# A graph network on one core: two small loads change their places in SP's order

## The chip, the cores and the metric

The kernel runs on 1 core of one Trainium2 chip. The metric is device time in microseconds of one execution, median of several; less is better.

## The reference

Two graph layers over 6250 nodes with 128 features and 106,250 edges (sorted by destination, both directions of 50,000 random pairs, and a loop at each node):

```python
h = max(layernorm(x), 0)
msg = edge_weight * (h @ W_i [dst] + h @ W_j [src] + edge_attr @ W_e)
x = x + segment_sum(msg, dst) + h @ W_self
h = max(layernorm(x), 0)
for W_l, b, W_r in two layers:          # relu between them, log_softmax behind the second
    mean = segment_sum(h[src], dst) / max(count(dst), 1)
    h = mean @ W_l.T + b + h @ W_r.T
out = x + h
```

## The kernel before

Nodes are laid out in 49 blocks of 128 (BLOCKS), worked on in 7 steps of 7 blocks (STEPS, UNROLL), a step in a part of 4 and one of 3 blocks.

The edge phase runs over 64 chunks of 1664 edges. GpSimd gathers source rows, VectorE builds one-hot matrices, TensorE sums them by destination (L1030). On the way TensorE also counts, for every group of destinations, how often each source occurs (L1039); ScalarE copies the counts and SP stores them in DRAM (`counts`, L502). The degree and the sum of edge weights of every node go to `node_rows` (L490). For each block the product h @ W_i (the "own" rows) is stored in `own_rows` (L494).

Then comes the passage in which this case's change lies. A node's own row has to be multiplied by its sum of edge weights. SP loads the sums as 49 rows of 128 values (L512) into `node_weight_rows`, TensorE transposes them (L1127), ScalarE copies them to `node_weight` (L865). SP loads the own rows back in two parts, of 2 and of 5 steps (`OWN_PARTS`, L517; 7168 and 17,920 B in each of 128 partitions), and GpSimd multiplies them block by block (L684, 49 instructions). For each step VectorE adds the own rows (L1537) and TensorE's mix (L931, added by L1542) to x and works out the layer norm (L1231, L1234); ScalarE normalizes (L720) and makes the high halves in f16 (L727), VectorE the low halves (L1522); TensorE turns the rows (L920). On TensorE L1127 stands ahead of all mixes. On VectorE this is `first_rows`; behind it stand the maximum and the reciprocal of the degrees (L1620, L1622, semaphore `inv_made`). SP stores the reciprocals in `inv_row` (L535), waits for the store and loads them back broadcast to 128 partitions (L527, `load_inverse`).

The two passes of the second layer (PASSES 1 and 2) don't gather. Each multiplies the node features by the stored counts in 18 "supers" of 98 matmuls (L1120, `sum_super`): super k needs 4287.5 KB of counts in `ring[k % 2]` (L523, `load_counts`), and behind it VectorE scales the sums by `inv_deg[k % 2]` (L1582, `keep_sums`). `ring[0]` and `deg_lines` lie where the gathered rows were; `ring[1]` and both `inv_deg` lie over the accumulators that the mixes read, so they wait for the last mix (`mixed[0]` at 49). For k from 2 on, SP issues the counts when super k - 2 has ended and the inverse when VectorE has read it. Behind super 0 of pass 1 TensorE turns the last two steps (L1135), VectorE copies them (L1349), and super 1 waits for these copies and for its counts.

SP issues every load and store of this passage in program order, each behind its waits.

Of the kernel before, what the change touches and what calls it, by code (L numbers as in the profile page):

```python
# [5 lines left out]
P = 128  # L6
NODES, EDGES, FEATS = 6250, 106250, 128
BLOCKS = -(-NODES // P)
USED = BLOCKS * P
TILES = 13  # L10
CHUNK = P * TILES
CHUNKS = -(-EDGES // CHUNK)
# [101 lines left out]
def gnn_program(nc, x, src, src_batches, dst, dst_lines, prev_lines, src_lines, factor_lines, edges, weights, biases, out):  # L114
# [12 lines left out]
    def scratch(name, shape, dt=f32):  # L127
        return nc.dram_tensor(name, shape, dt, kind="Internal").ap()
# [5 lines left out]
    node_rows = scratch("node_rows", (2, COUNTED * NCHUNK))  # L134
# [8 lines left out]
    with ctx:  # L143
# [6 lines left out]
        def sem(name):  # L150
            return ctx.enter_context(nc.semaphore(name))
# [29 lines left out]
        def carve(home, taken, width, dt=f32, partitions=P):  # L181

            taken[0] += width
            assert taken[0] <= home.shape[1]
            part = home[0:partitions, taken[0] - width:taken[0]]
            return part if dt is f32 else part.bitcast(dt)
# [41 lines left out]
        in_h, in_N = [0], [0]  # L228
# [7 lines left out]
        w_half = carve(accN, in_N, P // 2, f16)  # L236
        own_h = [carve(accN, in_N, FEATS) for _ in range(2)]
        own_hT = carve(accN, in_N, P)
        assert in_N[0] <= USED
        node_weight_rows = accN[0:BLOCKS, USED:USED + P]  # L240
        def ghot(k):
            at = k * GW
# [89 lines left out]
        weight_in, weight_turned, weight_kept = sem("weight_in"), sem("weight_turned"), sem("weight_kept")  # L332
# [28 lines left out]
        node_out = [sem(f"node_out{b}") for b in range(2)]  # L361
# [14 lines left out]
        mixed = [sem(f"mixed{p}") for p in range(3)]  # L376
# [42 lines left out]
        def _(sp):  # L419
# [52 lines left out]
            for i, c in enumerate(ORDER):  # L472
                b = i % 2
# [13 lines left out]
                if c < COUNTED:  # L487
# [4 lines left out]
                    t = i - OWN_MADE  # L492
# [14 lines left out]
            fast = sp.value_load(fast_row[0:1, 0:1], min_val=0, max_val=1)  # L507
            with sp.If(fast):

                for b in range(2):  # L510
                    sp.wait_ge(node_out[b], 16 * (CHUNKS // 2 - b))
                sp.dma_start(node_weight_rows, node_rows[0, 0:USED].rearrange("(t p) -> t p", p=P)).then_inc(weight_in, 16)  # L512
                sp.wait_ge(own_out, 16 * BLOCKS)
                sp.wait_ge(piece_done, DSUPERS * PIECES)
                for n, (lo, hi) in enumerate(OWN_PARTS):
                    columns = slice(lo * UNROLL * FEATS, hi * UNROLL * FEATS)
                    sp.dma_start(accN[:, columns], own_rows[:, columns]).then_inc(own_back[n], 16)  # L517

                for h in range(2):
                    sp.wait_ge(counts_out[h], 16 * COUNTED)  # L520
                sp.dma_start(deg_lines, node_rows[1, :].rearrange("(p n) -> p n", p=LINES)).then_inc(deg_in, 16)
                def load_counts(p, k):
                    sp.dma_start(ring[k % 2].rearrange("p (c n) -> p c n", c=SUPER),  # L523
                                 counts[k * SUPER:(k + 1) * SUPER, :, :].rearrange("c p n -> p c n")).then_inc(ring_in[p][k % 2], 16)

                def load_inverse(p, k):
                    sp.dma_start(inv_deg[k % 2], inv_row[k * SNODES:(k + 1) * SNODES].rearrange("(a n) -> a n", a=1)  # L527
                                 .to_broadcast([P, SNODES])).then_inc(inv_in[p][k % 2], 16)

                sp.wait_ge(added[0], ADDED)  # L530
                load_counts(1, 0)
                sp.wait_ge(mixed[0], BLOCKS)
                load_counts(1, 1)
                sp.wait_ge(inv_made, 2)
                sp.dma_start(inv_row.rearrange("(p n) -> p n", p=LINES), deg_lines).then_inc(inv_out, 16)  # L535
                sp.wait_ge(inv_out, 16)
                for p in PASSES:
                    if p == 1:
                        load_inverse(1, 0)
                        load_inverse(1, 1)  # L540
                    else:

                        sp.wait_ge(super_done[1], SUPERS - 1)
                        load_counts(2, 0)
                        sp.wait_ge(super_read[1], SUPERS + 1)
                        load_inverse(2, 0)
                        sp.wait_ge(super_done[1], SUPERS)
                        load_counts(2, 1)
                        sp.wait_ge(super_read[1], SUPERS + 2)
                        load_inverse(2, 1)  # L550
                    for k in range(2, SUPERS):

                        sp.wait_ge(super_done[p], k - 1)
                        load_counts(p, k)
                        sp.wait_ge(super_read[p], k + 1)
                        load_inverse(p, k)
# [659 lines left out]
        def _(dve):  # L1216
# [137 lines left out]
            def load_window(c):  # L1354
                _, (more, base) = nc.values_load_multi_w_load_instructions(
                    win_row[0:1, bass.ds(c, 1), :].rearrange("a c n -> a (c n)"), engines=[dve.engine], min_val=0, max_val=NODES - 1,
                    skip_runtime_bounds_check_because="both were clamped to these bounds when the row was written")
                dve.reg_mov(next_more, more)
                dve.reg_mov(next_base, base)
# [76 lines left out]
            def window_base(c):  # L1436
                _, (base,) = nc.values_load_multi_w_load_instructions(
                    win_row[0:1, c, 1:2], engines=[dve.engine], min_val=0, max_val=NODES - 1,
                    skip_runtime_bounds_check_because="it was clamped to these bounds when the row was written")
                return base  # L1440
# [342 lines left out]
```

## Time and profile before

| | us |
|---|---|
| median of 3 executions | 1657.07 |
| lowest, highest | 1655.46, 1662.93 |
| the profiled execution | 1655.46 |
| its span, first to last instruction | 1653.7 |
| TensorE (PE) busy | 1416.1 |
| VectorE (DVE) busy | 977.2 |
| GpSimd (POOL) busy | 727.3 |
| ScalarE (ACT) busy | 601.3 |

The profile shows one execution. Times in rows are microseconds from the span's start unless marked ns. PE is TensorE, PEld its weight loads, DVE VectorE, ACT ScalarE, POOL GpSimd; SPq is the queue from which SP issues transfers. L12 is line 12 of the kernel.

### The profile page before, as it was taken

The page shows a single profiled execution, that of the slowest core. Times are in us where ns is not written, and L with a number is a line of the kernel's source. Part 1 is how long each engine was busy: PE and PEld are TensorE (multiplying, and loading weights), DVE is VectorE, ACT ScalarE, POOL GpSimd, SP SyncE. Part 2 cuts the span into 40 slices and gives each one's busy share as a digit, 9 for nine tenths or more (in the row PEclk, how much of TensorE's full clock was granted, in tenths as well). Part 3 has the DMA queues.
Part 4 walks back from the last instruction along what each step waited for, and adds up shares of the span by engine and source line. Part 5 has one row for each costly group of instructions (what it writes and reads, how often), then busy time and mean ns, then how long its engine had stood idle before and what let it go on. Part 6 is the DMA issues. An engine that isn't in the chain of part 4 may idle for free.

```text
span 1653.7 us, 25952 instructions
## 1 busy us (share of the span) xinstructions
PE 1416.1 (86%) x8448; PEld 1011.7 (61%) x8449; DVE 977.2 (59%) x4423; ACT 601.3 (36%) x1479; POOL 727.3 (44%) x783
## 2 busy tenths in 40 slices
PE   2587787888887988979899777899999979999997
PEld 0365666666665766657566556566666656666664
DVE  7798988898897987979799566300101130010204
ACT  5356556655646465554544234300000010020203
POOL 8777755665767766677677768000000000000000
PEclk9688988999998999989899899999999989999999
DMA  8467767988998888888799864586767647777773
GB/s 268 145 221 270 256 241 252 328 283 268 303 312 281 286 300 265 289 295 290 260 319 322 253 214 189 227 309 263 301 262 301 262 186 289 271 309 269 304 275 137
DMA packets 178853, 441.26 MB, mean 267 GB/s; under 512 B 24619, under 2 KB 104924, under 8 KB 175388
## 3 DMA queue, kind: packets, MB, share of 16 engines
q1 hardware_dynamic: 155996, 391.75, 65.5%
q0 software_dynamic: 22432, 46.97, 10.4%
q8 instruction: 70, 1.15, 0.3%
q10 hardware_dynamic: 288, 0.85, 0.1%
q14 instruction: 67, 0.55, 0.1%
HBM read 318.94 MB, written 120.55 MB: 266 GB/s over the span
## 4 chain that ended last, share of the span: by engine, by line
PE 60%; POOL 10%; DVE 9%; DMA 8%; ACT 7%; issue 4%; SPq 1%; DVEq 0%; POOLq 0%; ACTq 0%
PE psAE L1120 32%; PE psAE L1030 13%; POOL home L630 8%; DMA home<-h_table 6%; PE psAE L1062 4%; ACT home L789 3%; PE psW L931 3%; DVE home L1420 3%; DVE home L1424 2%; PE psW L1049 2%; PE psW L1039 2%; DVE home L1478 2%; ACT home L821 1%; DMA counts<-home 1%; PE psNS L1039 1%
## 5 line engine op out<-in xcount | busy, mean ns | idle before, releaser
L630 POOL DMA_INDIRECT home<-h_table,src_i x676 | 654.6, 968 | 289.4 <-issue 199.0
L1120 PE MATMUL psAE<-home 128*128 128x350 f16 x3528 | 538.1, 313 | 5.7 <-DVE home L1522 3.7
L1120 PEld LDWEIGHTS psAE<-home 128*128 128x128 f16 x3528 | 337.8, 96 | 200.9 <-issue 3.7
L1030 PE MATMUL psAE<-home 128*128 128x256 f32 x1352 | 331.4, 405 | 45.9 <-DMA home<-h_table,src_i 24.7
L1030 PEld LDWEIGHTS psAE<-home 128*128 128x128 f32 x1352 | 274.1, 205 | 102.8 <-issue 55.9
L1478 DVE TENSOR_SCALAR home<-iota_h,dst_rel,home 128x128 f32<-128x128 f16 x832 | 221.4, 361 | 30.4 <-PE psAE L1030 27.9
L789 ACT ACTIVATE home<-psW 128x490 f16<-128x490 f32 x418 | 211.5, 577 | 59.3 <-PE psW L1039 33.6
L1420 DVE TENSOR_SCALAR home<-iota_h,tile 128x245 f16<-128x245 f16 x1004 | 208.8, 298 | 30.1 <-PE psW L1049 16.5
L1424 DVE TENSOR_SCALAR home<-iota_h,tile 128x128 f16<-128x128 f16 x1004 | 178.3, 278 | 0.0
L1039 PE MATMUL psW<-home 128*128 128x245 f16 x836 | 126.9, 283 | 38.1 <-DVE home L1424 35.6
L1582 DVE SCALAR_TENSOR_TENSOR home<-psAE,home 128x350 f32<-128x350 f32 x18 | 9.4, 523 | 242.9 <-PE psAE L1120 238.1
L1582 DVE SCALAR_TENSOR_TENSOR home<-psAE,unscale,home 128x350 f32<-128x350 f32 x18 | 10.5, 581 | 238.4 <-PE psAE L1120 238.4
L1062 PE MATMUL psAE<-home 128*128 128x400 f32 x294 | 121.9, 561 | 26.0 <-DMA home<-h_table 25.8
L768 ACT ACTIVATE home<-psAE 128x256 f32<-128x256 f32 x52 | 20.0, 385 | 321.1 <-PE psAE L1030 321.1
L789 ACT ACTIVATE home<-psNS 128x490 f16<-128x490 f32 x212 | 110.4, 577 | 32.4 <-PE psNS L1039 22.5
L1039 PEld LDWEIGHTS psW<-home 128*128 128x128 f16 x836 | 80.1, 101 | 67.0 <-issue 26.7
L880 ACT ACTIVATE home<-home x14 | 8.0, 575 | 283.1 <-DVE home L1559 263.7
L1062 PEld LDWEIGHTS psAE<-home 128*128 128x128 f32 x294 | 59.4, 214 | 70.8 <-DMA home<-h_table 32.1
L1467 DVE TENSOR_SCALAR home<-iota_h,home 128x128 f16<-128x128 f16 x240 | 57.6, 327 | 54.7 <-PE psW L1049 43.8
L1039 PE MATMUL psNS<-home 128*128 128x245 f16 x424 | 68.0, 286 | 19.1 <-DVE home L1424 12.4
L821 ACT ACTIVATE home<-home 128x128 f16<-128x128 f16 x240 | 75.8, 393 | 0.0
L891 ACT ACTIVATE home<-home,shift (+1 forms) x49 | 18.9, 387 | 150.1 <-DVE shift L1589 150.1
(211 smaller groups left out, 1223.2 us busy)
## 6 DMA issues: line engine op xcount, KB each, us to landing
home<-counts SPq DMA_DIRECT2D x36, 4287.5 KB, 13.5
counts<-home SPq DMA_DIRECT2D x126, 612.5 KB
home<-edges SPq DMA_DIRECT2D x64, 845.0 KB
weighted<-home SPq DMA_DIRECT2D x24, 1225.0 KB
home<-weighted SPq DMA_DIRECT2D x36, 800.0 KB
home<-h_table,src_i POOLq DMA_INDIRECT x676
home<-h_table SPq DMA_DIRECT2D x36, 256.0 KB
home<-inv_row SPq DMA_DIRECT2D x36, 175.0 KB, 13.2
```

Source lines behind the costliest of these rows:

```text
L630: pool.indirect_dma_start(out=rows[to][:, j, :], out_offset=None, in_=from_table[:, :], in_offset=bass.IndirectOffsetOnAxis(ap=src_i[b][:, ...
L789: done = nc.scalar.activation(staged[h][:, :, at:at + 2 * GROUP], banks_of(i, "C", k)[u][:, 0:BCOLS].rearrange("p (d a) -> p a d", a=KEYS) ...
L821: done = nc.scalar.activation(whot_all[k % 2][:, j, 0, :], ghot(4 * k + j)[1], ACT.Copy, scale=w_parts[t][:, 0, at:at + 1])
L931: last = nc.tensor.matmul(bank[:, n * FEATS:(n + 1) * FEATS], frm[:, columns], w_sb[:, w, :], start=(k == 0), stop=(k == len(terms) - 1))
L1030: done = nc.tensor.matmul(psA[:, 0:2 * P].rearrange("p (n f) -> p n f", n=2), onehot[:, j, :], both_of(s, b, j), start=(j == 0), stop=(j = ...
L1039: done = nc.tensor.matmul(banks[j // 2][:, j % 2 * GCOLS:(j % 2 + 1) * GCOLS], residues, keys, start=True, stop=True)
L1062: done = nc.tensor.matmul(psE[:, 0:DNODES].rearrange("p (h d) -> p h d", h=2 * DSUPER), piece_h[b][:, a - n * PIECE, :], piece_w[b][:, :, ...
L1120: last = nc.tensor.matmul((psA, psE)[r][:, 0:SNODES].rearrange("p (c d) -> p c d", c=SUPER), halves[:, a, n, :], tiles[:, :, a, :], start= ...
L1420: nc.vector.tensor_scalar(ghot(k)[0], iota_h[:, 0:GCOLS], record_of(k, 0), None, ALU.is_equal)
L1424: last = nc.vector.tensor_scalar(ghot(k)[1], iota_h[:, 0:P], record_of(k, 2), None, ALU.is_equal)
L1467: last = nc.vector.tensor_scalar(whot_all[k % 2][:, j, 1, :], iota_h[:, 0:P], tile_of(t)[:, 2, at:at + 1], w_parts[t][:, 1, at:at + 1], AL ...
L1478: last = nc.vector.tensor_scalar(onehot[:, j, :], iota_h[:, 0:P], dst_rel[i % 2][:, j:j + 1], factor[i % 2][:, j:j + 1], ALU.is_equal, ALU ...
```

## The change

SP's order of issues in the passage changes in two places; no load, store, instruction or wait is added or dropped.

1. The load of the node weights, with its wait for the last stores of `node_rows`, moves from ahead of the two own-row loads to behind them.
2. For pass 1, the load of the counts of super 1, with its wait for the last mix, moves from ahead of the store of the inverse degrees to behind the first inverse load, so that the order is: inverse of super 0, counts of super 1, inverse of super 1.

An `assert` on the size of a region, which has no part in what runs, goes too.

```diff
@@ -236,7 +236,6 @@
-        assert in_N[0] <= USED
@@ -507,14 +506,14 @@
             with sp.If(fast):
 
-                for b in range(2):
-                    sp.wait_ge(node_out[b], 16 * (CHUNKS // 2 - b))
-                sp.dma_start(node_weight_rows, node_rows[0, 0:USED].rearrange("(t p) -> t p", p=P)).then_inc(weight_in, 16)
                 sp.wait_ge(own_out, 16 * BLOCKS)
                 sp.wait_ge(piece_done, DSUPERS * PIECES)
                 for n, (lo, hi) in enumerate(OWN_PARTS):
                     columns = slice(lo * UNROLL * FEATS, hi * UNROLL * FEATS)
                     sp.dma_start(accN[:, columns], own_rows[:, columns]).then_inc(own_back[n], 16)
+                for b in range(2):
+                    sp.wait_ge(node_out[b], 16 * (CHUNKS // 2 - b))
+                sp.dma_start(node_weight_rows, node_rows[0, 0:USED].rearrange("(t p) -> t p", p=P)).then_inc(weight_in, 16)
@@ -529,14 +528,14 @@
                 load_counts(1, 0)
-                sp.wait_ge(mixed[0], BLOCKS)
-                load_counts(1, 1)
                 sp.wait_ge(inv_made, 2)
                 sp.dma_start(inv_row.rearrange("(p n) -> p n", p=LINES), deg_lines).then_inc(inv_out, 16)
                 sp.wait_ge(inv_out, 16)
                 for p in PASSES:
                     if p == 1:
+                        sp.wait_ge(mixed[0], BLOCKS)
                         load_inverse(1, 0)
+                        load_counts(1, 1)
                         load_inverse(1, 1)
```

## Rows read from the trace of the kernel before

**Rows 1.** The page: span, and TensorE's busy time.

```profile
span 1653.7 us, 25952 instructions
PE 1416.1 (86%) x8448; PEld 1011.7 (61%) x8449; DVE 977.2 (59%) x4423; ACT 601.3 (36%) x1479; POOL 727.3 (44%) x783
```

**Rows 2.** Chain of waits, 985 to 1110 us: start, duration, what.

```profile
999.38 0.24 PE psAE L1127
...
999.96 8.76 POOL home L684 x14
1008.74 1.26 DVE x_sb L1537
...
1042.71 14.80 PE psAE L1120 x98
...
1060.46 0.56 DVE home L1349
1061.06 44.59 PE psAE L1120 x294
```

**Rows 3.** SP's issues, 984 to 1100 us: start, duration, line, transfer.

```profile
991.40 0.37 SPq L512 DMA_DIRECT2D home<-node_rows  x1
991.87 0.83 SPq L517 DMA_DIRECT2D home<-own_rows  x2
```

**Rows 4.** SP's issues, 1035 to 1060 us.

```profile
1039.91 0.38 SPq L523 DMA_DIRECT2D home<-counts  x1
1053.12 0.36 SPq L535 DMA_DIRECT2D inv_row<-home  x1
1054.60 0.83 SPq L527 DMA_DIRECT2D home<-inv_row  x2
1057.55 0.38 SPq L523 DMA_DIRECT2D home<-counts  x1
```

**Rows 5.** The two own-row loads (L517), from issue to landing.

```profile
DMA to landing us min/median/max: 5.9/8.4/10.9
```

**Rows 6.** All 36 counts loads (L523), from issue to landing.

```profile
DMA to landing us min/median/max: 13.0/13.5/15.0
```

**Rows 7.** Transfers issued from 1039 to 1042 us: KB, us to landing.

```profile
home<-counts SPq DMA_DIRECT2D x1, 4287.5 KB, 13.3
```

**Rows 8.** Transfers issued from 1054.5 to 1056 us.

```profile
home<-inv_row SPq DMA_DIRECT2D x2, 175.0 KB, 3.5
```

**Rows 9.** Transfers issued from 1058 to 1059 us.

```profile
home<-inv_row SPq DMA_DIRECT2D x1, 175.0 KB, 12.7
```

**Rows 10.** Packets by size, 992 to 993 us.

```profile
DMA packets 104, 0.22 MB, mean 216 GB/s; under 512 B 21, under 2 KB 66, under 8 KB 104
```

**Rows 11.** Packets by size, 993 to 996 us.

```profile
DMA packets 127, 0.88 MB, mean 292 GB/s; under 512 B 4, under 2 KB 8, under 8 KB 125
```

**Rows 12.** Packets by size, 1000 to 1001 us.

```profile
DMA packets 28, 0.50 MB, mean 502 GB/s; under 512 B 0, under 2 KB 0, under 8 KB 0
```

**Rows 13.** Packets by size, 1001 to 1002 us.

```profile
DMA packets 177, 0.24 MB, mean 237 GB/s; under 512 B 144, under 2 KB 144, under 8 KB 173
```

**Rows 14.** Windows between the passes: length, busy per engine, granted clock, DMA.

```profile
1344.00:1349.00 5.00, 0.94 (x4) 0.63 (x4) 2.20 (x7) 2.78 (x3) 0.00 (x0) 0.50 1.02 420
1349.00:1353.00 4.00, 4.00 (x17) 2.06 (x17) 4.00 (x5) 3.85 (x5) 0.00 (x0) 0.57 0.23 85
```

**Rows 15.** TensorE in order of time, 955 to 1045 us.

```profile
977.18 7.42 PE L1030 MATMUL psAE<-home 128*128 128x256 f32 x26 [4.91 <-DMA home<-h_table,src_i]
...
991.93 5.85 PE L1030 MATMUL psAE<-home 128*128 128x256 f32 x26 [3.13 <-DMA home<-h_table,src_i]
```

**Rows 16.** TensorE in order of time, 1040 to 1655 us.

```profile
1042.55 14.97 PE L1120 MATMUL psAE<-home 128*128 128x350 f16 x98
...
1059.11 0.98 PE L920 MATMUL psNS<-ident,home 128*128 128x128 f32 x7 [0.83 <-DVE home L1349]
...
1348.90 16.64 PE L1120 MATMUL psAE<-home 128*128 128x350 f16 x98 [3.69 <-DVE home L1522]
```

## Prediction

> **What bounds the kernel now.** I read the page first: TensorE is busy for 86% of a span of 1653.7 us [rows 1], so the question is where on TensorE's line the two edits fall. Both fall in the passage from the edge phase to the two passes over the stored counts, about 990 to 1076 us, and the chain of waits over that stretch says what releases what there [rows 2]. The transpose of the node weights on TensorE (L1127) runs at 999.38, GpSimd's multiplications of the own rows (L684) start at 999.96 and are the chain for 8.76 us (fourteen of them, the rows of the first two steps), VectorE takes over at 1008.74, and from there VectorE, ScalarE and TensorE hand each other seven steps until the first super starts at 1042.71. The second super starts at 1061.06, released by a copy on VectorE. After that TensorE runs supers of 14.8 us nearly back to back [rows 2, 16]. Whatever delays this passage is not won back later, because nothing behind it waits for anything but TensorE.
>
> Then the SP queue over the same stretch, since the edits only reorder SP's issues: node-weight load at 991.40, the two own-row loads from 991.87 [rows 3]; second counts load at 1039.91, the store of the inverse degrees at 1053.12, two inverse loads from 1054.60, third counts load at 1057.55 [rows 4]. Last, how long such loads take and in which order their packets run [rows 5 to 13].
>
> **Part 1: the node-weight load goes behind the own-row loads.** Nothing is added or removed; a load of 24.5 KB in 49 rows of 512 B is issued after 896 + 2240 KB instead of before them. All three conditions that SP waits for here are met before 991.4, so the waits themselves cost nothing in either order, and the own rows are issued 991.87 - 991.40 = 0.47 us earlier.
>
> What matters is when the small load lands. Packet sizes tell the order on the wire. From 992 to 993 there are 66 - 21 = 45 packets of 512 B to 2 KB, nearly all of the 49 rows of the node weights, while the own rows were already issued [rows 10]; from 993 to 996 nearly all packets are under 8 KB, the first own load with 7168 B a row [rows 11]; from 1000 to 1001 none is [rows 12], the second own load with 17,920 B a row; and the 200 B rows of the degree load, issued at 993.89, appear only from 1001 to 1002 [rows 13]. A small load waits for the large ones in front of it. The same is seen later: an inverse load lands 3.5 us after its issue on a free queue [rows 8] and 12.7 us behind a counts load [rows 9]. The own loads took 5.9 and 10.9 us [rows 5]; the second was issued at the end of a pair that took 0.83 us, about 992.3, and so landed at 1003.2. In the new order it lands some 0.5 us sooner, 1002.7, and the 49 rows, about a third of a microsecond of extra time, at about 1003.0. TensorE's L1127 then goes at about 1003.1 instead of 999.38: **3.7 us**. Queued behind it on TensorE is the whole first mix; behind it in data are ScalarE's copy, GpSimd's 49 multiplications and so VectorE. VectorE's second step is bound by GpSimd [rows 2], so nothing takes the delay up: the first super starts 3.7 us later. Bounds: nothing below 2.5 if the order on the wire holds (own packets end near 1001.0, less 0.5, plus 1 for the rows and 1 from last packet to landing), 4.5 above; 0 if it does not hold (a rival, below).
>
> The Trainium skill ("DMA: Bandwidth & Descriptors", "Why a DMA increments its semaphore by 16 and not by 1" and "Queues, rings and completion order") says that a load is spread over the largest number of engines up to 16 that divides its slowest dimension, which for 49 rows would be 7, and that completion isn't first in, first out per issuing engine. By that rule the small load could land ahead of the second own load, as soon as seven engines are through with their shares; an estimate by the page would be 1 us less than the 3.7. The trace agrees with ring order in [rows 10 to 13] and can't show which engines are used.
>
> **Part 2: the second counts load goes behind the inverse degrees.** Before, it is issued at 1039.91 and lands 13.3 us later [rows 4, 7], at 1053.2, 7.9 us ahead of its use at 1061.06. Afterwards SP first waits for VectorE's reciprocal, stores the row, waits for the store, issues one inverse load and only then the counts load, in the place that the second inverse load has now: the pair starts at 1054.60 and takes 0.83 us, so at about 1055.05. On a queue that is empty but for one inverse load it lands no sooner than 13.0, likely in 13.3 us [rows 6, 7]: 1055.05 + 13.3 = 1068.35. TensorE starts the second super 0.1 us later, at 1068.4 instead of 1061.06: **7.3 us**. Cover of 7.9 us is used up and 15.1 us of lateness is put in. All these times also carry part 1's 3.7 us, so the two add up.
>
> What is late next: the second inverse load, behind the counts load, is needed at the end of the second super, 15 us later, and lands at about 1069. The third counts load is issued at 1057.55 as now, runs behind the second for another 10.5 us or so and lands near 1080, before the second super can end at 1083. From there the queue is as before. VectorE's copies of the turned blocks and the first inverse load keep their times. The store L535 now finds a free queue, which it all but had. All of this costs nothing.
>
> **TensorE's clock.** TensorE ends the turns at 1060.1 [rows 16] and now idles 8.3 us. After the idle stretch between the passes the granted clock was 0.50 before and 0.57 for four microseconds after the restart, that is largely the 1.2 GHz level [rows 14], and that super took 16.64 us against 14.97 at full clock [rows 16]; after an idle of 4.9 us in the edge phase 26 matmuls took 7.42 against 5.85 us [rows 15]. So the second super loses **1.7 us** (bounds 0 and 1.7: nothing, if the clock holds). The idle of 4 to 5 us ahead of L1127 also may slow the first mixes; VectorE turns to the second mix only behind GpSimd's fourteen products, 1008.74 - 999.38 = 9.4 us after L1127, so I put it at 0, with 0.5 as the upper bound. The slow stretch at 1015 to 1021 may shift by as much either way.
>
> **Sum.** 3.7 + 7.3 + 1.7 = 12.7 us. The profiled execution took 1655.46 us (span 1653.7 and 1.8 around it) and is the lowest of three; its sum is 1668.2. Their median is 1657.07, 1.6 higher, which gives 1669.8. I forecast 1669.0.
>
> **Rivals.**
> - Both delays happen (the forecast): 0.80. With bounds: 2.5 + 7.0 + 0 = 9.5 to 4.5 + 7.5 + 2.2 = 14.2 us, that is 1665.0 on the profiled execution's scale to 1671.3 on the median's.
> - The node weights slip past the own rows and land before 999.38, by the rule cited or because the rows find a free engine. Then only 7.3 + 1.7 = 9.0 us remain, 7.3 without the clock's share: 1662.8 to 1666.1. For it speaks only that the small load is small; against it [rows 9, 10, 13]. 0.11.
> - The second and third counts loads share the engines instead of following each other. They are issued 2.5 us apart, so the second would land up to 8 us later: 20 us in all, 1676. [Rows 12, 13] show the loads one after the other, against it. 0.05.
> - The other side, faster: the counts load at 1039.91 runs through the first super; if it slows TensorE's and VectorE's accesses there, taking it away gives time back. The place is 1041 to 1053. The first super took 14.97 us with it, and its 98 matmuls run at 14.8 us in the chain [rows 2, 16], so they are not seen to be slowed. It decides only if it returns more than the 12.7 us lost out of a super of 15 us, and 8.3 more for faster by over 0.5%; if a super could run in no time at all, 12.7 - 14.8 would give 1655. 0.02.
> - The remaining 0.02 is for no effect: the counts load lands within 6.0 us of 1055.05, where the shortest of 36 took 13.0 [rows 6]; 1657.
>
> **How the numbers follow.** A measurement of this kernel tells about 0.5%, 8.3 us, from no change: 1665.4 is the border. The forecast case lies over it but for its lowest corner; the second straddles it, the third lies over it. Slower 0.80 x 0.98 + 0.11 x 0.5 + 0.05, about 0.89; within 0.5% 0.09; faster 0.02. The range takes in the second case's bottom and the forecast's top, and 2 or 3 us above for runs like the highest of the three: 1663 to 1674. Given the likeliest case alone I would say 1665 to 1672.
>
> **What the new profile would show.** Right: L1127 on TensorE near 1003, after an idle ended by a transfer; GpSimd's L684 starting 0.6 us later; first super about 3.7 us late; the second counts load issued near 1058.7 and landing after some 13.3 us; an idle of TensorE of about 8 us ended by a transfer from the counts, and a second super of 16.6 us; from the third super on everything late by the same 12.7 us. Wrong: L1127 at its old time (part 1's ring order), a landing of the counts load over 16 us (shared engines), or a second super of 15.0 us (clock).

## The result and the profile after

| | before | after |
|---|---|---|
| median of 6 executions, us | 1659.59 | 1673.70 |
| lowest, highest | 1655.17, 1665.42 | 1669.33, 1679.89 |
| the profiled execution, its span | 1655.46, 1653.7 | 1664.25, 1662.4 |

The ratio is 1.0081 with a 95% interval of 1.0053 to 1.0109: slower by 13.4 us (8.8 to 18.1). The kernel after is one line shorter, so its lines from 239 on carry smaller numbers, by 1 in most of what follows: L1126 is the old L1127, L1119 the old L1120.

The profiled execution of after is only 8.7 us longer than that of before. The reason lies ahead of the change: its edge phase ended 9.6 us sooner, the last turn of sums (old L1005, new L1004) being at 988.70 and not at 998.26. This end of the edge phase moves by some 20 us between executions of all the kernels below, so I count from there. Page of after:

```profile
span 1662.4 us, 25953 instructions
PE 1418.8 (85%) x8448; PEld 1013.4 (61%) x8449; DVE 979.4 (59%) x4423; ACT 600.4 (36%) x1479; POOL 727.2 (44%) x783
```

SP's issues of after, in order of time. They answer to [rows 3, 4]: own rows first, then the node weights; counts of super 1 only behind the store and the first inverse load.

```profile
985.21 0.85 SPq L513 DMA_DIRECT2D home<-own_rows  x2
986.15 0.36 SPq L516 DMA_DIRECT2D home<-node_rows  x1
...
1050.91 0.34 SPq L532 DMA_DIRECT2D inv_row<-home  x1
1052.37 0.36 SPq L526 DMA_DIRECT2D home<-inv_row  x1
1052.76 0.43 SPq L522 DMA_DIRECT2D home<-counts  x1
...
1057.19 0.38 SPq L522 DMA_DIRECT2D home<-counts  x1
```

TensorE of after, in order of time; in brackets the idle time before a row and what ended it.

```profile
988.70 0.44 PE L1004 MATMUL psAE<-ident,home 128*128 128x128 f32 x2 [0.47 <-ACT home L767]
996.32 0.34 PE L1126 MATMUL psAE<-ident,home 49*128 49x49 f32 x1 [7.18 <-DMA home<-node_rows]
...
1040.61 16.55 PE L1119 MATMUL psAE<-home 128*128 128x350 f16 x98
1057.00 0.93 PE L919 MATMUL psNS<-ident,home 128*128 128x128 f32 x7
1058.55 0.98 PE L919 MATMUL psNS<-ident,home 128*128 128x128 f32 x7 [0.62 <-DVE home L1348]
1068.19 42.09 PE L1119 MATMUL psAE<-home 128*128 128x350 f16 x268 [8.66 <-issue]
```

The same places in before:

```profile
998.26 0.44 PE L1005 MATMUL psAE<-ident,home 128*128 128x128 f32 x2 [0.47 <-ACT home L768]
999.38 0.23 PE L1127 MATMUL psAE<-ident,home 49*128 49x49 f32 x1 [0.68 <-issue]
...
1061.06 44.59 PE L1120 MATMUL psAE<-home 128*128 128x350 f16 x294 [0.96 <-DVE home L1349]
```

Both waits that were forecast are there. TensorE idles 7.18 us for the node weights (0.68 before, for nothing in particular), and 8.66 us ahead of super 1, where it idled 0.96. The second idle time is put down to "issue", but the transfers name it. Transfers issued from 1052.7 to 1053.1 us of after, with the time to landing:

```profile
home<-counts SPq DMA_DIRECT2D x1, 4287.5 KB, 15.3
```

1052.76 + 15.3 = 1068.06, and super 1 starts at 1068.19. The wire order of part 1 shows too. Packets of after from 994 to 995 us, then from 995 to 996:

```profile
DMA packets 28, 0.45 MB, mean 449 GB/s; under 512 B 1, under 2 KB 3, under 8 KB 3
```

```profile
DMA packets 251, 0.28 MB, mean 281 GB/s; under 512 B 162, under 2 KB 209, under 8 KB 249
```

Up to 995 it is the 17,920 B packets of the own rows; from 995 to 996 there are 209 - 162 = 47 packets of 512 B to 2 KB, the node weights, and L1126 follows at 996.32. Four windows of after: window, length, busy time of PE, PEld, DVE, ACT and POOL, then the granted clock (third number from the right), DMA share and GB/s:

```profile
1036.00:1040.00 4.00, 0.30 (x3) 0.28 (x3) 3.88 (x13) 3.96 (x9) 0.00 (x0) 1.00 0.01 2
1040.00:1044.00 4.00, 4.00 (x19) 2.31 (x18) 1.84 (x11) 3.31 (x9) 0.00 (x0) 0.57 0.00 0
1060.00:1068.10 8.10, 0.00 (x0) 0.00 (x0) 0.43 (x1) 0.00 (x0) 0.00 (x0) 0.56 0.99 404
1068.10:1072.00 3.90, 3.81 (x16) 2.10 (x17) 0.00 (x0) 0.00 (x0) 0.00 (x0) 0.60 1.02 419
```

Super 1 starts at a clock of 0.60, mostly the 1.2 GHz level. So does super 0 (0.57), which takes 16.55 us and not 14.97 as in [rows 16]. That of super 0 isn't the change's doing, as the experiments show: it is slow in most profiles of either order.

### The profile page after: what moved, and what is told of

The parts are those of the page before. It is cut to its first block and busy times, and to the rows that moved or that the text cites. A ratio compares the mean times of both kernels' runs of the same rounds, so it can differ in the third digit from the quotient of the medians.

```text
span 1662.4 us, 25953 instructions
## 1 busy us (share of the span) xinstructions
PE 1418.8 (85%) x8448; PEld 1013.4 (61%) x8449; DVE 979.4 (59%) x4423; ACT 600.4 (36%) x1479; POOL 727.2 (44%) x783
## 5 line engine op out<-in xcount | busy, mean ns | idle before, releaser
L1119 PE MATMUL psAE<-home 128*128 128x350 f16 x3528 | 541.3, 314 | 13.4 <-issue 8.7
L1119 PEld LDWEIGHTS psAE<-home 128*128 128x128 f16 x3528 | 339.1, 96 | 210.5 <-issue 12.6
L1029 PE MATMUL psAE<-home 128*128 128x256 f32 x1352 | 331.6, 406 | 44.1 <-DMA home<-h_table,src_i 20.1
L1477 DVE TENSOR_SCALAR home<-iota_h,dst_rel,home 128x128 f32<-128x128 f16 x832 | 222.6, 364 | 30.3 <-PE psAE L1029 27.8
L1419 DVE TENSOR_SCALAR home<-iota_h,tile 128x245 f16<-128x245 f16 x1004 | 208.9, 301 | 30.1 <-PE psW L1048 16.4
L1038 PE MATMUL psNS<-home 128*128 128x245 f16 x424 | 66.7, 282 | 21.5 <-DVE home L1423 18.5
L930 PE MATMUL psW<-w_sb,home 128*128 128x128 f32 x588 | 72.7, 284 | 0.8 <-DVE home L1581 0.8
## 6 DMA issues: line engine op xcount, KB each, us to landing
home<-counts SPq DMA_DIRECT2D x36, 4287.5 KB, 13.7
home<-inv_row SPq DMA_DIRECT2D x36, 175.0 KB, 13.5
```

What stands on the lines that cost most here:

```text
L930: last = nc.tensor.matmul(bank[:, n * FEATS:(n + 1) * FEATS], frm[:, columns], w_sb[:, w, :], start=(k == 0), stop=(k == len(terms) - 1))
L1029: done = nc.tensor.matmul(psA[:, 0:2 * P].rearrange("p (n f) -> p n f", n=2), onehot[:, j, :], both_of(s, b, j), start=(j == 0), stop=(j = ...
L1038: done = nc.tensor.matmul(banks[j // 2][:, j % 2 * GCOLS:(j % 2 + 1) * GCOLS], residues, keys, start=True, stop=True)
L1119: last = nc.tensor.matmul((psA, psE)[r][:, 0:SNODES].rearrange("p (c d) -> p c d", c=SUPER), halves[:, a, n, :], tiles[:, :, a, :], start= ...
L1419: nc.vector.tensor_scalar(ghot(k)[0], iota_h[:, 0:GCOLS], record_of(k, 0), None, ALU.is_equal)
L1477: last = nc.vector.tensor_scalar(onehot[:, j, :], iota_h[:, 0:P], dst_rel[i % 2][:, j:j + 1], factor[i % 2][:, j:j + 1], ALU.is_equal, ALU ...
```

## The experiments

Four stretches of the profiled executions tell more than the total. A is from the last turn of sums (L1005) to the node-weight transpose (L1127); B from there to super 0; C from the start of super 0 to the end of super 1 (SP issues a counts load at that moment); D is the rest. All in us, worked out as differences of starts.

| profiled execution | A | B | C | D | sum | ratio of times, 95% interval |
|---|---|---|---|---|---|---|
| before | 1.1 | 43.2 | 33.5 | 577.6 | 655.4 | |
| after | 7.6 | 44.3 | 44.0 | 577.8 | 673.7 | 1.0081 (1.0053 to 1.0109) |
| e1_weights_behind_own | 4.6 | 44.8 | 33.5 | 578.3 | 661.3 | 1.0043 (1.0021 to 1.0064) |
| e2_counts_behind_inverse | 1.2 | 44.1 | 44.3 | 577.8 | 667.4 | 1.0060 (1.0028 to 1.0092) |
| e3_weights_on_act_queue | 2.2 | 44.2 | 35.0 | 577.3 | 658.8 | 1.0035 (1.0015 to 1.0055) |
| e4_reciprocal_early | 1.1 | 44.0 | 34.6 | 578.6 | 658.4 | 1.0004 (0.9979 to 1.0028) |
| e5_idle_filled | 7.6 | 44.0 | 44.4 | 577.6 | 673.6 | 1.0081 (1.0052 to 1.0111) |
| e6_weights_between | 2.4 | 44.7 | 35.0 | 577.9 | 659.9 | 1.0005 (0.9981 to 1.0029) |
| e7_weights_behind_counts | 17.4 | 44.0 | 34.4 | 578.5 | 674.2 | 1.0070 (1.0046 to 1.0095) |
| e8_weights_act_queue_early | 2.1 | 44.8 | 35.0 | 577.6 | 659.4 | 1.0009 (0.9985 to 1.0033) |
| e9_idle_filled_36 | 8.0 | 44.3 | 43.2 | 578.3 | 673.8 | 1.0079 (1.0059 to 1.0098) |
| e10_first_step_on_vector | 1.2 | 41.4 | 33.5 | 578.4 | 654.5 | 0.9980 (0.9966 to 0.9995) |
| e11_reciprocal_early_and_vector | 1.1 | 40.1 | 34.5 | 578.7 | 654.4 | 0.9982 (0.9969 to 0.9995) |

All ratios are to before, run on the same chip. The chip of the last three runs took 2013.9 us for before (some 350 us more, all of it in the edge phase); only ratios and stretches are compared there.

**One edit at a time.** e1 has only the first edit, e2 only the second, as in the diff of the change.

> The first edit alone: the node-weight load behind the own-row loads, the counts of super 1 loaded early as before. Theory: transfers that SP issues run in order, so the 49 small rows wait for 3136 KB; TensorE idles ahead of L1127 until they land. L1127 runs 6 to 8 us after the last turn of sums (L1005) instead of 1.1 us; first super later by that and up to 1 us for the clock; super 1 starts 3.7 us behind the end of super 0 as before. Sum 4 to 8 us over before, ratio 1.002 to 1.005. Rival (the small load slips past): L1127 1.1 us behind L1005, ratio 1.000.

> The second edit alone: counts of super 1 behind the first inverse load, node weights in front as before. Theory: the load starts some 13 to 15 us later, its cover of 7.9 us is gone, TensorE idles about 8 us ahead of super 1, which then takes 16.4 us instead of 14.97 for the clock. L1127 1.1 us behind L1005. Sum 7.3 + 1.5 = 8.8 us over before, ratio 1.005. Rival (the second and third counts loads share the engines): landing over 16 us and ratio 1.01 or more. Rival (the load is covered anyway): 0.

TensorE of e1, in order of time:

```profile
997.57 0.44 PE L1005 MATMUL psAE<-ident,home 128*128 128x128 f32 x2 [0.48 <-ACT home L768]
1002.19 0.34 PE L1127 MATMUL psAE<-ident,home 49*128 49x49 f32 x1 [4.18 <-DMA home<-node_rows]
```

TensorE of e2:

```profile
1005.14 0.44 PE L1005 MATMUL psAE<-ident,home 128*128 128x128 f32 x2 [0.47 <-ACT home L768]
1006.29 0.23 PE L1127 MATMUL psAE<-ident,home 49*128 49x49 f32 x1 [0.70 <-issue]
...
1078.20 32.01 PE L1120 MATMUL psAE<-home 128*128 128x350 f16 x201 [8.45 <-issue]
```

Each edit brings its own wait and not the other's. By ratio e1 costs 7.2 us (3.5 to 10.7) and e2 10.0 us (4.7 to 15.3); together that is 17 against 13.4 measured for both, well within the intervals. In e1's profile L1127 comes 4.6 us behind L1005, 3.5 us more than in before, and not the 6 to 8 that I had read off after's profile.

**How far behind must the node weights be?** e6 puts their load between the two own loads, e7 behind the counts of super 0 too.

```diff
+# e6: inside the loop over OWN_PARTS, behind the own load of part 0
+if n == 0: wait node_out; sp.dma_start(node_weight_rows, ...)
...
 load_counts(1, 0)
+# e7: here instead
+wait node_out; sp.dma_start(node_weight_rows, ...)
```

> The node-weight load between the two own-row loads. Theory of order within the queue: it waits for 896 KB, not for 3136, and lands about 5 us sooner than behind both, near 6 us after its issue, which is at or before L1127's turn in executions where the last gather comes late. Cost against before 0 to 2 us, ratio 1.000 to 1.001; L1127 at most 2.5 us behind L1005. Rival (any place behind a large load costs the same, or none does): as the first edit alone, or as before.

> The node-weight load behind the counts load of super 0 as well. Theory of order within the queue: it waits for 4287.5 KB more and lands 14 to 16 us after the counts are issued, so L1127 stands 15 to 16 us behind L1005, and the time is 14 to 16 us over before, ratio 1.009. Rival (a small load slips past large ones): it lands 2 to 3 us after its issue, L1127 3 to 4 us behind L1005, ratio 1.001 to 1.002.

TensorE of e6 (lines up by one), then of e7:

```profile
1003.99 0.26 PE L1128 MATMUL psAE<-ident,home 49*128 49x49 f32 x1 [1.94 <-DMA home<-node_rows]
```

```profile
1018.51 0.34 PE L1127 MATMUL psAE<-ident,home 49*128 49x49 f32 x1 [16.91 <-DMA home<-node_rows]
```

SP's issues of e7:

```profile
1002.20 0.40 SPq L520 DMA_DIRECT2D home<-counts  x1
1002.69 1.49 SPq L531 DMA_DIRECT2D home<-node_rows  x1
```

24.5 KB issued at 1002.69 are used at 1018.51, 15.8 us later: the rival of a small load that slips past is dead within SP's queue. The load is used 6.0 us after its issue in e6 (issued at 998.00), 10.2 in after (986.15 to 996.32), 15.8 in e7, in step with the bytes ahead. The time of e7 is a miss in size: 11.7 us over before (7.7 to 15.8) where 14 to 16 were expected and stretch A shows 16.2, just outside the interval. The profiled execution doesn't explain it: the counts took 16.1 us to land there, and 14.3 (e3, e4) to 18.9 us (after) for the same load of super 0 in the other profiles, depending on how much of the own rows was still on the wire.

**Another queue.** In e3 and e8 ScalarE issues the load, in e3 behind its last copy of sums, in e8 ahead of it, once the last counts are stored:

```diff
+if i == CHUNKS - 1:  # e8, ahead of ScalarE's keep_sums; e3: at the head of ScalarE's last If(fast)
+    act.wait_ge(node_out[b], ...), act.wait_ge(counts_out[b], 16 * COUNTED)   # e3: node_out alone
+    act.dma_start(node_weight_rows, ...).then_inc(weight_in, 16)
```

> Own rows as in the first edit, but the node weights are loaded by ScalarE on its own queue behind its last copy of sums, a little before the last turn of sums. The own rows are then still on the wire. Theory of order within SP's queue: from another queue the load doesn't wait for them and lands 2 to 3 us after its issue, so L1127 stands 2 to 4 us behind L1005, and the time is 1 to 3 us over before, ratio 1.001. Rival (the 16 engines are full, whatever the queue): L1127 waits as in the first edit alone, 6 to 8 us, ratio 1.002 to 1.005.

> Own rows in SP's queue as in the first edit; the node weights are loaded by ScalarE on its own queue as soon as the last counts have been stored and ahead of its last copy of sums, about 2 us after SP has issued the own rows and while these are on the wire. Theory (the wait is for the same queue's order): the 512 B packets run among the own rows' packets, the load lands within 3 us of its issue, L1127 stands 1.1 us behind L1005, ratio 1.000. Rival (the engines are full, whatever the queue): the 512 B packets run behind the own rows, and L1127 is late as in the first edit alone, ratio 1.002 to 1.005.

ScalarE and TensorE of e8, in order of time:

```profile
1005.05 0.57 ACTq L841 DMA_DIRECT2D home<-node_rows  x1
```

```profile
1011.30 0.44 PE L1010 MATMUL psAE<-ident,home 128*128 128x128 f32 x2 [0.47 <-ACT home L765]
1013.37 0.26 PE L1132 MATMUL psAE<-ident,home 49*128 49x49 f32 x1 [1.62 <-DMA home<-node_rows]
```

Packets of e8 from 1009 to 1010 us:

```profile
DMA packets 35, 0.44 MB, mean 436 GB/s; under 512 B 0, under 2 KB 11, under 8 KB 11
```

e3 decided nothing: in the profiled execution the last gather came so late that the own rows had landed. In e8 they were on the wire (their second load landed 12.0 us after its issue at about 1001.2, at 1013.2), and the small packets did run among theirs, 11 in the microsecond shown, but the load was used 8.3 us after its issue and ended together with them. So my theory was half wrong: it isn't only the order within SP's queue. Another queue let the small packets in between, and yet the load was done no sooner than the large one. That e8's time is 1.0009 proves no gain over e1 (their intervals overlap); its L1005 came late, which hides the wait. The queue of ScalarE moved 56 packets for the 49 rows. The Trainium skill ("DMA: Bandwidth & Descriptors", "Why a DMA increments its semaphore by 16 and not by 1") has such a load on 7 engines, each with one more write for the semaphore, and 49 + 7 = 56 agrees with it. Its "Queues, rings and completion order" has each engine take turns between the queues, a packet at a time, and gives such a packet as typically 9 to 17 descriptors. The turns are in the trace, but here one lasts a single row. The small packets come in seven series, one of them with starts at 1009.03, 1009.72, 1010.41 and 1011.09, 0.69 us apart, and a 17,920 B packet takes 0.67 us: each small packet sat out a large one, as long as large ones were left.

**What holds the second edit's load back.** e4 has the second edit, and VectorE makes the reciprocals in the fourth step of the first layer:

```diff
-# behind first_rows: wait deg_in; max with 1; reciprocal
+if s == 3:  # in first_rows, behind the own rows' addition
+    wait deg_in; max with 1; reciprocal
```

> The second edit, but VectorE makes maximum and reciprocal of the degrees within the fourth step of the first layer, not behind the seventh. Theory: what delays the counts in the second edit is the wait for the reciprocal; with it out of the way the store, the inverse load and the counts load follow the last mix at about 1040, the counts land near 1054, ahead of super 1, and the whole cost of the second edit goes: ratio 1.000, within 1 us, perhaps 0.3 us faster since the first inverse is there when super 0 ends. Rival (it is the place in the queue behind store and inverse load that costs): TensorE idles ahead of super 1 as before, ratio 1.005.

SP's issues of e4, in order of time:

```profile
1029.61 0.36 SPq L533 DMA_DIRECT2D inv_row<-home  x1
1047.39 0.34 SPq L527 DMA_DIRECT2D home<-inv_row  x1
1047.77 0.43 SPq L523 DMA_DIRECT2D home<-counts  x1
```

The order of the loads is the edit's, but the counts are issued 4.2 us ahead of super 0 (1051.98) and not 12.2 us into it, and the cost is gone: 1.0004 (0.9979 to 1.0028). So what costs is the wait for the reciprocal in front of them. The same profile answers why the load took 15.3 us in after and not 13.3 as in [rows 7]. Transfers issued from 1047.5 to 1048.2 us of e4:

```profile
home<-counts SPq DMA_DIRECT2D x1, 4287.5 KB, 14.9
```

In e4 the next counts are issued only at 1068.27, long after this landing, so sharing the engines with them isn't the reason. What e4, e2 (15.5) and after have in common is one inverse load right ahead. Packets of e4 from 1049 to 1050 us:

```profile
DMA packets 53, 0.09 MB, mean 90 GB/s; under 512 B 6, under 2 KB 46, under 8 KB 53
```

40 of its 128 packets of 1400 B are in this microsecond, 55 in the one before at 77 GB/s, and only 7 packets of the counts run by 1050; they pass 370 GB/s at 1051.5, 3.7 us after the issue, where in before they do so 2.1 us after it (1042.0). So I put the difference down to the inverse load; no run has this order of loads without it. It is no law of landings: other counts loads took 13.0 to 14.9 us with a free wire. The third counts load of after took 22.4 us, behind the second, and landed at 1079.6, ahead of its use at 1084.6.

**The clock.** e5 and e9 are the kernel after with 48 and 36 extra matmuls of 350 columns ahead of super 1's wait, results dropped:

```diff
+if p == 1 and k == 1:
+    for _ in range(48):  # e9: 36
+        nc.tensor.matmul(psB[2][:, 0:SNODES], halves[:, 0, 0, :], ...)
 pe.wait_ge(ring_in[p][r], (k // 2 + 1) * 16)
```

> Both edits, and TensorE runs 48 matmuls of 350 columns into an unused bank (extra work, its result is dropped) ahead of its wait for the counts of super 1. Theory of the clock: the idle stretch is filled, so super 1 runs at full clock, 15.0 us instead of 16.4; its start stays where the counts land. About 1.4 us under both edits, ratio 1.007. Rival (the slow super 1 comes from its transfers, not from the idle time): super 1 still takes 16.4 us.

> Both edits, and 36 instead of 48 extra matmuls (results dropped) ahead of TensorE's wait for the counts of super 1, so that they end before the counts land. Theory of the clock: from the end of super 0 to the end of super 1 it takes 26.0 to 26.3 us, where both edits alone took 27.45 and 48 extra matmuls 27.8; super 1 at 15.0 us; time 1.2 us under both edits, ratio about 1.007, not to be told from 1.0081 by time alone. Rival (the slow super 1 isn't from the idle time): super 1 at 16.4 us.

TensorE of e5, then of e9, in order of time:

```profile
1074.35 8.71 PE L1113 MATMUL psW<-home 128*128 128x350 f16 x48 [0.96 <-DVE home L1351]
1082.89 7.41 PE L1122 MATMUL psAE<-home 128*128 128x350 f16 x48
```

```profile
1420.67 6.97 PE L1113 MATMUL psW<-home 128*128 128x350 f16 x36 [0.96 <-DVE home L1351]
1428.15 44.59 PE L1122 MATMUL psAE<-home 128*128 128x350 f16 x294 [0.51 <-DMA home<-counts]
```

The last row of e5 breaks off where the view ends. With 48, super 1 takes 15.0 us (1082.89 to SP's issue at 1097.89), but starts late, 29.35 us behind the start of super 0 where after has 27.58, and nothing is won. The store of the inverse degrees took 1.2 us longer to land in this execution, and the extra matmuls ended some 0.6 us behind the landing of the counts. With 36 the fill ends 0.5 us before the counts land, super 1 starts with them and takes 15.0 us, against 1084.61 - 1068.19 = 16.4 in after. So the 1.4 us are the idle time's. Stretch C is 0.8 us shorter than after's; the store of the inverse degrees took 0.7 us longer to land in this execution. The time, 1.0079, can't show it.

**A version that beats both.** B begins with GpSimd's 8.76 us [rows 2]. In e10 (order of loads as before) VectorE, idle there, does the first step itself; e11 adds this to e4.

```diff
-dve.wait_ge(own_scaled, 7); x_rows = x_rows + accN
+for t in range(UNROLL):  # first step only; GpSimd starts with the second
+    nc.vector.scalar_tensor_tensor(out=x_sb[:, t, :], in0=accN[...t], scalar=node_weight[:, t:t + 1],
+                                   in1=x_sb[:, t, :], op0=ALU.mult, op1=ALU.add)
```

> The order of loads as before the change; VectorE itself multiplies and adds the own rows of the first step (7 fused instructions), GpSimd begins with the second. Theory: GpSimd's 8.76 us at the head of the first layer are what the node weights' landing releases, and shortening them shortens the passage: from L1127 to the first super 40.5 to 42 us instead of 43.2 to 44, ratio 0.9985. Rival (VectorE and ScalarE bind the seven steps whatever GpSimd does): the same 43 to 44 us, ratio 1.000.

> The last one together with the early reciprocal (and the second edit's order of loads). Theory: both gains add, 2 to 3 us under before, ratio 0.998 to 0.999. Rival: 1.000 as the early reciprocal alone gave.

TensorE of e10, in order of time:

```profile
1353.07 0.23 PE L1127 MATMUL psAE<-ident,home 49*128 49x49 f32 x1 [0.71 <-issue]
...
1394.47 14.96 PE L1120 MATMUL psAE<-home 128*128 128x350 f16 x98
```

41.4 us instead of 43.2 to 44.8, and 40.1 in e11. Both kernels are faster than before, by 0.2% (0.05 to 0.34%); the early reciprocal adds nothing to the time.

## Why the prediction was right, and where a size was off

- **Part 1, 3.7 us.** The mechanism is right (e1, e6, e7). The size is right for an execution like before's, and e1's profile has 3.5. (The lower bound isn't what its working gives: 1001.0 - 0.5 + 1 + 1 is 1002.5, and less 999.38 that is 3.1 and not 2.5.) But the size isn't a constant. In all four executions with the load behind both own parts and nothing more, it was used 11.1 to 11.5 us after the first own issue (e1 990.67 to 1002.19, after 985.21 to 996.32, e5 998.20 to 1009.54, e9 1344.17 to 1355.58). TensorE reached its last turn of sums 6.9, 3.5, 3.7 and 3.4 us after that issue, depending on the last gather. The cost is the difference, less the 1.1 us that pass anyway: 3.5 in e1 and 6.5 to 6.9 in the others, over my upper bound of 4.5. The wait has cover, and the cover varies by more than the cost: over all profiles the last turn of sums comes 3.4 us (e9, e10) to 13.5 us (e3) after SP's first issue here, and with 13.5 nothing is left to wait for. The completion order that the prediction cited, with 1 us to gain, hardly matters: by the semaphore updates in the traces the small load was complete 0.09, 0.20 and 0.05 us ahead of the second own load in after, e1 and e9, and 0.14 us behind it in e5. The updates also show what [rows 10 to 13] couldn't: seven follow one another as the data land, so the load did run on seven engines.
- **Part 2, 7.3 us.** The path through reciprocal, store, inverse load and counts load is right (e2, e4). The counts were issued 12.15 us after super 0's start, 12.5 forecast. The step that was mis-sized is the landing "in 13.3 us": 14.9 to 15.5 in every profile with an inverse load right ahead, 13.3 to 13.6 for the same load in the seven profiles with the old order (before, e1, e3, e6, e7, e8, e10). From super 0's start, super 1 came at 27.6 us in after and 27.8 in e2; 18.5 in before. That is 9.1 to 9.3 us. Where super 0 itself is slow, as in e3 and e6 (super 1 at 19.9), the same edit costs 7.6 to 7.9, since the transfers don't wait for TensorE.
- **Clock, 1.7 us.** 1.4 by after and e9. That the idle ahead of L1127 costs nothing can't be told: B is 44.0 to 44.8 in executions with and without that idle (e4 and e2 without, 44.0 and 44.1).
- **Sum.** 12.7 forecast, 13.4 by the ratio. By stretches 673.7 - 655.4 = 18.3, of which 1.6 are super 0's clock and 1.1 are B. In both, before's profile was better than most: super 0 is slow in most profiles of either order, and B is 44 in e2 and e4 as well. That leaves 15.6: 6.5 + 7.5 + 1.4 and 0.2 in D. The single profile thus overstates part 1's mean.
- **Luck.** That 12.7 comes so near to 13.4 is in part luck. Against before's own profile, with super 0 at full clock, part 2 costs 9.1 us and not 7.3; against an execution with a slow super 0 it costs 7.5 to 7.9. A landing put 2 us too short and a first super that was faster than most cancel. The time itself, 1673.70, is 4.7 us over the 1669.0, above the 1665 to 1672 of the likeliest case and 0.3 us below the top of the range; 2.5 us of this are that before took 1659.59 this time and not 1657.07.
- **The rivals.** Node weights that slip past: excluded by e7 within one queue. Shared engines: excluded, by e4's landing. A first super that gains from a free wire: excluded. At the low clock it took 16.61 and 16.62 us in e6 and e8, with the load running through it, and 16.61 and 16.55 in e2 and after, without.
- What stays open: why e3 took 0.35% more than before by time, where its profile has little to show for it (with an earlier last gather its load would meet the own rows on the wire as in e8, which no run shows); why the time of e7 rose by 11.7 us and not by 16; why e8's small packets began to run only 4.0 us after their issue (1005.05 to 1009.03).

## What to carry to other kernels

A transfer's place in its queue is part of its cost: read packet sizes by the microsecond to see what a small but urgent load stands behind, and put it in front of large ones that are needed later. A prefetch must not be issued behind a wait for something that it doesn't need; e4 kept the new order and lost nothing once that wait was short. When a wait ends on the later of two things that vary by several microseconds, state the cost as a difference of the two, not as a number from one profile.

## What the runs showed of the hardware

Behind an inverse load of 175 KB in 1400 B packets the 4287.5 KB of super 1 took 14.9 to 15.5 us to landing and not 13.3 to 13.6. Its packets began at 77 to 90 GB/s on the wire, where the counts run at about 420. A 24.5 KB load on ScalarE's queue took 8.3 us to its use while SP's queue was full, and 1.8 us in e3, where it was empty (1009.61 to 1011.37).

Super 0 took 14.96 to 14.97 us in three of the profiles and 16.0 to 16.6 in the ten others, behind the same order of work on TensorE. The first four microseconds of super 0 in e1, then in e8 (the granted clock is the third number from the right):

```profile
1047.00:1051.00 4.00, 4.00 (x29) 2.55 (x28) 1.36 (x5) 3.84 (x9) 0.00 (x0) 1.00 1.02 421
1058.10:1062.10 4.00, 4.00 (x18) 2.10 (x17) 1.37 (x5) 3.82 (x9) 0.00 (x0) 0.57 1.02 423
```

Full clock and mostly the 1.2 GHz level, both with 3.54 us of idle time ahead of the last turns before super 0. After (0.57) had 3.70 there, e10 (full clock) 3.60. What decides between the two levels no run here shows.
